# GNN edge stage on one Trainium2 core: gather indices copied mid-pair behind a tile-sum wait, first edge layer for two quads at once

## The chip, the cores and the metric

One core of a Trainium2 chip. The metric is the device time of one launch in microseconds (us), lower is better; it is the median of several runs. One execution was also taken by the hardware profiler. The core's engines run side by side, each with an instruction queue of its own, and meet only at semaphores: TensorE (PE; its weight loads are shown apart as PEld), VectorE (DVE), ScalarE (ACT), GpSimd (POOL) and SyncE (SP, which only issues DMA transfers). "Queue" rows such as ACTq or SPq are DMA issues of that engine.

## The reference

A graph layer over N = 12,500 nodes of 160 features (64 scalars, 32 vectors of 3) and E = 400,000 edges sorted by destination, then a residual and a layer norm. Everything is float32. What costs time are the edges:

```python
h_s, h_v = (node features) @ lin1                       # per node, (12500, 160) in all
w  = silu(edge_scalars @ fc_w1 / 8) @ fc_w2 / 8         # per edge: 64 -> 64 -> 224
es, ev = h_s[edge_src], h_v[edge_src]                   # gather of 160 values per edge
m_s1 = w1 * es * e0                                     # products of w, the gathered row
m_s2 = w4 * einsum('eci,ei->ec', ev, e1) / sqrt(3)      # and the edge's four attributes
m_v1, m_v2, m_v3 = (w2*es) x e1, w3*ev*e0, w5*cross(ev, e1)
agg = segment_sum(messages, edge_dst)                   # per node
out = layernorm(x + gated(lin2(agg) + sc(x)))
```

## The kernel before

The program has three blocks, one after the other. The set-up block computes the table of transformed node rows (`m.h`) in HBM and prepares constants. The edge block goes over all edges and leaves sums per destination window in `m.agg`. The node block turns these into the output. The change touches the edge block alone.

**Tiles, quads, pairs.** Edges are padded to 3128 tiles of 128. Four tiles are a quad (`QT = 4`, 782 quads), two quads a pair (391 pairs), four pairs a round of the ring (`RING = 8` quads of buffers for gathered rows; `ROUNDS = 97` rounds and a rest of six quads). Nothing is scheduled automatically: each engine's queue is the order in which its function below is written, with waits on counting semaphores.

**GpSimd** (`pair`, L543 to L555) works by pairs. It waits until the products of the pair that used these ring slots before are done (`prod_ready`), copies the 8 columns of source indices of the pair into `idx` (L549), waits for that copy's own semaphore `idx_ready`, and issues eight indirect gathers of 128 rows x 160 values (L553), each into one tile's slot of `rows`.

**TensorE** (`turn`, L777 to L784) works by quads q: `hidden(q + 2)` is the first edge layer (L744, 128 x 256: two tiles stand on the upper half of the partitions and two on the lower, with a block-diagonal `fc1`), into its half b of PSUM tile `psx`; `weights(q + 1)` is the second layer (L753, two products of 480 columns) into `psw[b]`; `combine(q - 1)` (L772, L774) adds the tile sums of two quads into one window (`psg`); `sum_tiles(q)` (L762) sums products over the edges of a tile into eight destinations (`pst`). It takes quad q's products and so waits for `prod_ready`, and ends with `tiles_summed`.

**ScalarE** (`turn`, L607 to L613) applies silu to `psx` (L590, `hid`), issues the load of the edge features two quads on into the half of `es` that is free (L584), copies the combined window out of PSUM (L600, `aggsb`) and the tile sums (L605, `tsum`).

**VectorE** (`products`, L660 to L679) waits for the second layer (`w_ready`) and for the quad's four gathers (`rows_loaded`), and multiplies them (L480, L490, L491 into `prod`); it also makes the selection matrices (`sel`, `hot`, `shifts`). **SyncE** stores the windows to HBM.

In the edge block, each fp32 matmul stands as two records in the trace. At the block's beginning ScalarE also issues eight loads of the edge columns `e_cols` (L620), between the first loads of `es` and the ones after it.

Of the kernel before, what the change touches and what calls it, by code (L numbers as in the profile page):

```python
# [398 lines left out]
def edge_block(nc, io, m):  # L399

    with ExitStack() as ctx:
# [6 lines left out]
        es = sb("es", [P, 2, CH])  # L408
        hid = sb("hid", [P, 2, CH])
# [19 lines left out]
        psx = ctx.enter_context(nc.psum_tensor("psx", [P, 2, 256], F32))  # L429
# [4 lines left out]
        es_loaded = [sem(f"es_loaded{b}") for b in range(2)]  # L434
# [4 lines left out]
        prod_seen = sem("prod_seen")  # L439
# [54 lines left out]
        def _(sp):  # L494
# [23 lines left out]
            with sp.Else():  # L518
# [5 lines left out]
                def tile(q, u, first):  # L524
                    if not first:
                        sp.wait_ge(g_added, 16 * (QT * q + u))
                        sp.sem_inc(loads_seen, 1)
                    h = S * (u % 2)
                    sp.dma_start(es[0:S, 0, 0:P], io["esP"][h:h + S, ds(q * CH + P * (u // 2), P)]).then_inc(g_es, 16)
                    sp.dma_start(dstrow[:], io["dst"][ds(QT * q + u, 1), :].to_broadcast([P, P])).then_inc(g_dst, 16)  # L530
# [9 lines left out]
        def _(pool):  # L540
            miss = pool.value_load(m.misses[0:1, 0:1], min_val=0, max_val=CHECKS * P)

            def pair(I, v, free):  # L543

                q = I * RING + 2 * v
                if free:
                    pool.wait_ge(prod_ready, q + 2 - RING)
                    pool.sem_inc(prod_seen, 1)
                nc.gpsimd.tensor_copy(idx[:, 2 * QT * v:2 * QT * v + 2 * QT], m.src[:, ds(q * QT, 2 * QT)]).then_inc(idx_ready, 1)  # L549
                pool.wait_ge(idx_ready, RING // 2 * I + v + 1)  # L550
                pool.sem_inc(prod_seen, 1)
                for j in range(2 * QT * v, 2 * QT * v + 2 * QT):
                    nc.gpsimd.indirect_dma_start(  # L553
                        out=rows[:, j, :], out_offset=None, in_=m.h,
                        in_offset=bass.IndirectOffsetOnAxis(ap=idx[:, j:j + 1], axis=0)).then_inc(rows_loaded[j // QT], 16)  # L555

            with pool.If(miss == 0):
                for v in range(RING // 2):
                    pair(0, v, False)
                with pool.Fori(1, ROUNDS) as I:  # L560
                    for v in range(RING // 2):
                        pair(I, v, True)
                for v in range(REST // 2):
                    pair(ROUNDS, v, True)
# [15 lines left out]
        def _(act):  # L580
            miss = act.value_load(m.misses[0:1, 0:1], min_val=0, max_val=CHECKS * P)
            def load(q, b):

                act.dma_start(es[:, b, :], io["esP"][:, ds(q * CH, CH)]).then_inc(es_loaded[b], 16)  # L584
# [22 lines left out]
            def turn(i, b, last, free, ahead, following):  # L607
                q = 2 * i + b
                if ahead:
                    activate(q + 2, b, True, following)  # L610
                if last:
                    copy_out(q - 1, i - 1 + b, 1 - b, free)
                copy_tiles(q, b)  # L613

            with act.If(miss == 0):
                for b in range(2):
                    load(b, b)
# [3 lines left out]
                for b in range(2):  # L621
                    activate(b, b, False, True)
# [12 lines left out]
            with act.Else():  # L635
# [3 lines left out]
                with act.Fori(0, TILES) as t:  # L639
                    act.wait_ge(g_hid, t + 1)  # L640
                    nc.scalar.activation(hid[0:S, 0, 0:P], psx[0:S, 0, 0:P], ACT.Silu,
# [94 lines left out]
        def _(pe):  # L736
            miss = pe.value_load(m.misses[0:1, 0:1], min_val=0, max_val=CHECKS * P)

            def hidden(q, i, b, free):

                pe.wait_ge(es_loaded[b], 16 * (i + 1))
                if free:
                    pe.wait_ge(hid_ready, q)
                nc.tensor.matmul(psx[:, b, 0:CH], m.fc1[:], es[:, b, :], start=True, stop=True).then_inc(hid_summed, 1)  # L744

            def weights(q, b, free):

                pe.wait_ge(hid_ready, q + 1)
                if free:
                    pe.wait_ge(prod_ready, q - 1)  # L750
# [398 lines left out]
```

## Time and profile before

| | |
|---|---|
| median of 3 runs | 4876.2 us (4875.2 to 4877.35) |
| the profiled execution | 4866.93 us |
| its span in the trace | 4865.1 us |
| edge block, first to last gather | 141.75 to 4409.43 us |
| busy: PE, POOL, DVE, ACT | 4238.8, 3066.4, 2525.6, 1760.2 us |

The page gives per engine the busy time and its share of the span; the waits view gives for each group of instructions how long its engine stood idle before it and what ended that idling ("issue" is time in which it waited for nothing that the profile shows); the timeline gives instructions in order of time, each with its start, its duration and, in brackets, the idle time before it and its releaser. Matmuls are pipelined and their ends are modelled, so TensorE's busy time is not its time at full speed; starts of matmuls can be compared with one another.

### The profile page before, as it was taken

The page shows a single profiled execution, that of the slowest core. Times are in us where ns is not written, and L with a number is a line of the kernel's source. Part 1 is how long each engine was busy: PE and PEld are TensorE (multiplying, and loading weights), DVE is VectorE, ACT ScalarE, POOL GpSimd, SP SyncE. Part 2 cuts the span into 40 slices and gives each one's busy share as a digit, 9 for nine tenths or more (in the row PEclk, how much of TensorE's full clock was granted, in tenths as well). Part 3 has the DMA queues.
Part 4 walks back from the last instruction along what each step waited for, and adds up shares of the span by engine and source line. Part 5 has one row for each costly group of instructions (what it writes and reads, how often), then busy time and mean ns, then how long its engine had stood idle before and what let it go on. Part 6 is the DMA issues. An engine that isn't in the chain of part 4 may idle for free. (4 is left out here: it accounts for less than half of the span.)

```text
span 4865.1 us, 80511 instructions
## 1 busy us (share of the span) xinstructions
PE 4238.8 (87%) x17609; PEld 1960.6 (40%) x17609; DVE 2525.6 (52%) x7615; ACT 1760.2 (36%) x5088; POOL 3066.4 (63%) x3529
## 2 busy tenths in 40 slices
PE   9888888888888888888888888888888888888996
PEld 7433333333333333333333333333333333335775
DVE  3455555555555555555555555555555555554556
ACT  2333333333333333333333333333333333332221
POOL 0677777777777777777777777777777777771000
PEclk9999999999999999999999999999999999999998
DMA  5533333333333333333333333333333333333434
GB/s 149 161 101 99 100 99 99 99 100 99 99 100 99 99 100 99 99 99 100 99 99 100 99 99 99 100 99 99 100 99 99 99 100 99 99 100 105 127 115 137
DMA packets 431352, 506.88 MB, mean 104 GB/s; under 512 B 71411, under 2 KB 359568, under 8 KB 430948
## 3 DMA queue, kind: packets, MB, share of 16 engines
q0 software_dynamic: 150144, 256.45, 20.4%
q1 hardware_dynamic: 152658, 133.76, 9.2%
q10 hardware_dynamic: 128530, 116.45, 7.9%
q8 instruction: 7, 0.11, 0.0%
q14 instruction: 13, 0.11, 0.0%
HBM read 426.32 MB, written 80.06 MB: 104 GB/s over the span
## 5 line engine op out<-in xcount | busy, mean ns | idle before, releaser
L553 POOL DMA_INDIRECT rows<-h_table,idx x3128 | 2987.5, 955 | 1201.2 <-issue 881.0
L480 DVE TENSOR_TENSOR prod<-psw,rows 128x384 f32<-128x384 f32 (+2 forms) x3128 | 1213.4, 450 | 1981.3 <-DMA rows<-h_table,idx 1918.5
L600 ACT ACTIVATE aggsb<-psg 32x160 f32<-32x160 f32 x3128 | 923.4, 295 | 2147.4 <-PE psg L774 2117.9
L753 PE MATMUL psw<-fc,hid 128*128 128x480 f32 x3128 | 1418.2, 577 | 0.0
L762 PE MATMUL pst_e<-prod,sel 128*32 128x448 f32 x6256 | 761.1, 559 | 537.3 <-DVE prod L491 537.1
L753 PEld LDWEIGHTS psw<-fc,hid 128*128 128x128 f32 x3128 | 607.5, 194 | 388.1 <-issue 344.7
L772 PE MATMUL psg<-tsum,shifts 128*128 128x448 f32 x1564 | 717.8, 541 | 1.6 <-ACT tsum L605 1.6
L774 PE MATMUL psg<-tsum,shifts 128*128 128x448 f32 x1562 | 715.3, 540 | 0.0
L744 PE MATMUL psx<-es,fc 128*128 128x256 f32 x1564 | 559.0, 440 | 18.6 <-DMA es<-in_esP 15.0
L762 PEld LDWEIGHTS pst_e<-prod,sel 128*32 128x32 f32 x6256 | 123.5, 108 | 1094.6 <-DVE prod L491 1052.8
L605 ACT ACTIVATE tsum<-pst_e 128x448 f32<-128x448 f32 x782 | 425.5, 544 | 348.6 <-PE pst_e L762 328.0
L744 PEld LDWEIGHTS psx<-es,fc 128*128 128x128 f32 x1564 | 237.0, 191 | 601.7 <-issue 585.1
L772 PEld LDWEIGHTS psg<-tsum,shifts 128*128 128x128 f32 x1564 | 300.1, 192 | 341.0 <-issue 337.8
L774 PEld LDWEIGHTS psg<-tsum,shifts 128*128 128x128 f32 x1562 | 297.1, 190 | 290.9 <-issue 290.9
L590 ACT ACTIVATE hid<-psx 128x256 f32<-128x256 f32 x782 | 299.7, 383 | 140.7 <-PE psx L744 96.9
L679 DVE TENSOR_TENSOR shifts<-shift,tile_offset 128x256 f32<-128x256 f32 x782 | 325.2, 416 | 0.0
L490 DVE TENSOR_TENSOR prod<-psw,rows 128x256 f32<-128x256 f32 x782 | 324.5, 415 | 0.0
L491 DVE TENSOR_TENSOR prod<-psw,rows 128x256 f32<-128x256 f32 x782 | 324.4, 415 | 0.0
L670 DVE TENSOR_TENSOR sel<-hot,e_cols 128x128 f32<-128x128 f32 x782 | 228.8, 293 | 53.0
L912 PE MATMUL pst<-ident,nag 128*32 128x128 f32 (+2 forms) x1764 | 186.7, 286 | 17.8 <-DMA nxv<-in_xT 17.0
L549 POOL COPY idx<-src_cols 128x8 int32 (+1 forms) x391 | 77.8, 199 | 141.2 <-issue 139.8
L912 PEld LDWEIGHTS pst<-ident,nag 128*32 128x32 f32 (+2 forms) x1764 | 120.5, 126 | 70.9 <-issue 23.2
(103 smaller groups left out, 1196.8 us busy)
## 6 DMA issues: line engine op xcount, KB each, us to landing
es<-in_esP ACTq DMA_DIRECT2D x782, 128.0 KB, 2.7
agg_table<-aggsb SPq DMA_DIRECT2D x782, 80.0 KB
rows<-h_table,idx POOLq DMA_INDIRECT x3128
nag<-agg_table SPq DMA_DIRECT2D x24, 1280.0 KB, 6.0
h_table<-hrow ACTq DMA_DIRECT2D x24, 320.0 KB, 3.7
nxr<-in_x SPq DMA_DIRECT2D x24, 320.0 KB, 6.7
out<-y SPq DMA_DIRECT2D x24, 320.0 KB
e_cols<-in_e4T ACTq DMA_DIRECT2D x8, 686.0 KB, 9.8
```

Source lines behind the costliest of these rows:

```text
L480: return nc.vector.tensor_tensor(out, w_part, ev, ALU.mult)
L490: nc.vector.tensor_tensor(w2, w[:, :, 0:S].rearrange(halves, c=V), vec[:, :, 0:S].rearrange(halves, c=V), ALU.mult)
L491: return nc.vector.tensor_tensor(out[:, :, V * B1A:V * B1A + S], w[:, :, S + 3 * V:WN], vec[:, :, 0:S], ALU.mult)
L553: nc.gpsimd.indirect_dma_start(out=rows[:, j, :], out_offset=None, in_=m.h, in_offset=bass.IndirectOffsetOnAxis(ap=idx[:, j:j + 1], axis=0 ...
L600: ins = nc.scalar.activation(aggsb[r, b, :], picked(psg[r, :], k), ACT.Copy)
L605: nc.scalar.activation(tsum[:, b, :], pst[b][:, 0:PW], ACT.Copy).then_inc(tsum_copied, 1)
L679: nc.vector.tensor_tensor(shifts[:, b, :, :, :].rearrange("p h k n -> p h (k n)"), m.shift[:].rearrange("p k n -> p (k n)").unsqueeze(1).t ...
L744: nc.tensor.matmul(psx[:, b, 0:CH], m.fc1[:], es[:, b, :], start=True, stop=True).then_inc(hid_summed, 1)
L753: ins = nc.tensor.matmul(both[:, 0:256 + WN], hid[:, b, P * c:P * c + P], m.fc2[:], start=True, stop=True)
L762: ins = nc.tensor.matmul(pst[b][W * j:W * j + W, 0:PW], sel[:, b, j, :, :], prod[:, b, j, :], start=True, stop=True, tile_position=(0, W * j))
L772: ins = nc.tensor.matmul(psg[:, 0:PW], shifts[:, b, 0, :, :], tsum[:, b, :], start=True, stop=not before)
L774: ins = nc.tensor.matmul(psg[:, 0:PW], shifts[:, b, 1, :, :], tsum[:, 1 - b, :], start=False, stop=True)
```

## The change

Two things change together.

On GpSimd, the index copy becomes a step of its own (`copy_indices`). The first pair's indices are copied before everything; those of each later pair are copied in the middle of the pair before it, after its fourth gather. The wait for products (`prod_ready`, of the quad seven back) is replaced by a wait for tile sums: before pair (q, q + 1), `tiles_summed` must have reached q - 2, that is, quad q - 3 must be summed on TensorE. The first two pairs don't wait for it.

The first edge layer handles two quads at once. `es`, `hid` and `psx` are no longer two halves of 256 columns but one piece of 512, numbered by r = q / 2. TensorE's `hidden(r)` is one product of 512 columns, in turns b = 0 only; ScalarE's `activate(r)` is one silu of 512 columns, likewise, and needs the second layer of quad 2r - 1 done, since `hid` has one buffer; one load brings the features of two quads. The second layer, the sums, the combining and all of VectorE stay by quads.

```diff
-        es = sb("es", [P, 2, CH])
-        hid = sb("hid", [P, 2, CH])
+        es = sb("es", [P, 2 * CH])
+        hid = sb("hid", [P, 2 * CH])
...
-            def pair(I, v, free):
-
-                q = I * RING + 2 * v
-                if free:
-                    pool.wait_ge(prod_ready, q + 2 - RING)
-                    pool.sem_inc(prod_seen, 1)
-                nc.gpsimd.tensor_copy(idx[:, 2 * QT * v:2 * QT * v + 2 * QT], m.src[:, ds(q * QT, 2 * QT)]).then_inc(idx_ready, 1)
+            def copy_indices(I, v):
+
+                slots = slice(2 * QT * v, 2 * QT * v + 2 * QT)
+                nc.gpsimd.tensor_copy(idx[:, slots], m.src[:, ds((I * RING + 2 * v) * QT, 2 * QT)]).then_inc(idx_ready, 1)
+
+            def pair(I, v, following, early):
+
+                if not early:
+                    pool.wait_ge(tiles_summed, I * RING + 2 * v - 2)
                 pool.wait_ge(idx_ready, RING // 2 * I + v + 1)
-                pool.sem_inc(prod_seen, 1)
-                for j in range(2 * QT * v, 2 * QT * v + 2 * QT):
+                pool.sem_inc(order_seen, 1)
+                for j in range(2 * QT):
+                    slot = 2 * QT * v + j
                     nc.gpsimd.indirect_dma_start(
...
+                    if following and j == QT - 1:
+                        last = v == RING // 2 - 1
+                        copy_indices(I + 1 if last else I, 0 if last else v + 1)
...
-            def activate(q, b, free, following):
-                act.wait_ge(hid_summed, q + 1)
+            def activate(r, free, following):
+
+                act.wait_ge(hid_summed, r + 1)
                 if free:
-                    act.wait_ge(w_ready, q - 1)
-                nc.scalar.activation(hid[:, b, :], psx[:, b, 0:CH], ACT.Silu, scale=HID ** -0.5).then_inc(hid_ready, 1)
+                    act.wait_ge(w_ready, 2 * r)
+                nc.scalar.activation(hid[:], psx[:], ACT.Silu, scale=HID ** -0.5).then_inc(hid_ready, 1)
                 if following:
-                    load(q + 2, b)
+                    load(r + 1)
...
-                if ahead:
-                    activate(q + 2, b, True, following)
+
+                if ahead and b == 0:
+                    activate(i + 1, True, following)
...
-            def hidden(q, i, b, free):
-
-                pe.wait_ge(es_loaded[b], 16 * (i + 1))
+            def hidden(r, free):
+
+                pe.wait_ge(es_loaded, 16 * (r + 1))
                 if free:
-                    pe.wait_ge(hid_ready, q)
-                nc.tensor.matmul(psx[:, b, 0:CH], m.fc1[:], es[:, b, :], start=True, stop=True).then_inc(hid_summed, 1)
+                    pe.wait_ge(hid_ready, r)
+                nc.tensor.matmul(psx[:], m.fc1[:], es[:], start=True, stop=True).then_inc(hid_summed, 1)
...
-                if hid_following:
-                    hidden(q + 2, i + 1, b, True)
+                q = 2 * i + b
+                if b == 0 and hid_following:
+                    hidden(i + 1, True)
```

GpSimd's queue within the ring loop, the second pair of a round, before (`idx<-src_cols` is the index copy, `rows<-h_table,idx` a gather, REGISTER_ALU and ISA rows are steps of the sequencer):

```order
L547 REGISTER_ALU
L549 ISA [waits prod_ready]
L549 COPY idx<-src_cols 128x8
L550 REGISTER_ALU
L553 DMA rows<-h_table,idx 128x160 [waits idx_ready]
L553 DMA rows<-h_table,idx 128x160 x7
```

and the same pair now:

```order
L552 REGISTER_ALU [waits tiles_summed]
L556 DMA rows<-h_table,idx 128x160 [waits idx_ready]
L556 DMA rows<-h_table,idx 128x160 x3
L546 ISA
L546 COPY idx<-src_cols 128x8
L556 DMA rows<-h_table,idx 128x160 x4
```

The copy has moved from directly ahead of the gather that waits for it to five places ahead of the next pair's first gather, and both waits now stand together at the beginning of the pair.

TensorE's queue in its loop, the turn b = 0 and the beginning of b = 1, before (`psx` first layer, `psw` second, `psg` combining, `pst_e` tile sums):

```order
L743 ISA [waits es_loaded0]
L744 MATMUL psx<-es,fc 128x256 [waits hid_ready]
L753 MATMUL psw<-fc,hid 128x480 [waits prod_ready,hid_ready]
L753 MATMUL psw<-fc,hid 128x480
L771 REGISTER_ALU [waits shifts_ready,tsum_copied]
L772 MATMUL psg<-tsum,shifts 128x448 [waits agg_copied]
L774 MATMUL psg<-tsum,shifts 128x448
L758 REGISTER_ALU
L762 MATMUL pst_e<-prod,sel 32x448 [waits tsum_copied,prod_ready]
L762 MATMUL pst_e<-prod,sel 32x448 x3
L743 REGISTER_ALU [waits es_loaded1]
L744 MATMUL psx<-es,fc 128x256 [waits hid_ready]
```

and now:

```order
L749 REGISTER_ALU [waits es_loaded]
L750 MATMUL psx<-es,fc 128x512 [waits hid_ready]
L756 REGISTER_ALU [waits hid_ready]
L760 MATMUL psw<-fc,hid 128x480 [waits prod_ready]
L760 MATMUL psw<-fc,hid 128x480
L778 REGISTER_ALU [waits shifts_ready,tsum_copied]
L779 MATMUL psg<-tsum,shifts 128x448 [waits agg_copied]
L781 MATMUL psg<-tsum,shifts 128x448
L765 REGISTER_ALU
L769 MATMUL pst_e<-prod,sel 32x448 [waits tsum_copied,prod_ready]
L769 MATMUL pst_e<-prod,sel 32x448 x3
L756 ISA [waits hid_ready]
```

The turn b = 0 begins with one product of 512 columns, and the turn b = 1 begins with the second layer directly.

## Rows read from the trace of the kernel before

**Rows 1.** The page's busy time, share of the span and instructions of each engine.

```profile
PE 4238.8 (87%) x17609; PEld 1960.6 (40%) x17609; DVE 2525.6 (52%) x7615; ACT 1760.2 (36%) x5088; POOL 3066.4 (63%) x3529
```

**Rows 2.** The page's granted TensorE clock in 40 slices, in tenths of full.

```profile
PEclk9999999999999999999999999999999999999998
```

**Rows 3.** Waits: engine, tile, line, releaser: us in total, times, longest.

```profile
DVE prod L480 <- DMA rows<-h_table,idx: 1918.5, 759, 4.5
POOL rows L553 <- issue: 881.0, 2735, 1.7
POOL rows L553 <- POOL idx L549: 319.7, 391, 1.0
POOL rows L553 <- DVE prod L491: 0.6, 2, 0.3
```

**Rows 4.** GpSimd's timeline at a pair's end: start us, duration us, [idle before].

```profile
2500.46 0.97 POOL L553 DMA_INDIRECT rows<-h_table,idx  x1 [0.82 <-POOL idx L549]
...
2510.18 0.20 POOL L549 COPY idx<-src_cols 128x8 int32 x1
2511.19 0.97 POOL L553 DMA_INDIRECT rows<-h_table,idx  x1 [0.81 <-POOL idx L549]
2512.46 0.95 POOL L553 DMA_INDIRECT rows<-h_table,idx  x1 [0.30 <-issue]
```

**Rows 5.** GpSimd's timeline: first pairs, a rare gap, the last gather.

```profile
141.75 0.19 POOL L549 COPY idx<-src_cols 128x8 int32<-128x8 int32 x1 [139.78 <-issue]
...
151.84 0.94 POOL L553 DMA_INDIRECT rows<-h_table,idx  x1 [0.30 <-issue]
...
163.51 0.20 POOL L549 COPY idx<-src_cols 128x8 int32<-128x8 int32 x1
...
2458.52 0.94 POOL L553 DMA_INDIRECT rows<-h_table,idx  x1 [1.67 <-issue]
...
4408.44 0.99 POOL L553 DMA_INDIRECT rows<-h_table,idx  x1 [0.30 <-issue]
```

**Rows 6.** Timeline of VectorE and TensorE behind the gather that ends at 2510.18.

```profile
2511.88 1.55 DVE L480 TENSOR_TENSOR prod<-psw,rows 128x384 f32<-128x384 f32 x4 [2.33 <-DMA rows<-h_table,idx]
...
2514.15 0.96 PE L762 MATMUL pst_e<-prod,sel 128*32 128x448 f32 x8 [0.42 <-DVE prod L491]
```

**Rows 7.** TensorE's timeline at the start of the edge block.

```profile
161.94 1.22 PE L744 MATMUL psx<-es,fc 128*128 128x256 f32 x2 [8.86 <-DMA es<-in_esP]
...
170.84 0.96 PE L762 MATMUL pst_e<-prod,sel 128*32 128x448 f32 x8
171.72 0.70 PE L744 MATMUL psx<-es,fc 128*128 128x256 f32 x2
172.26 1.77 PE L753 MATMUL psw<-fc,hid 128*128 128x480 f32 x4
173.87 0.92 PE L772 MATMUL psg<-tsum,shifts 128*128 128x448 f32 x2
...
175.47 0.96 PE L762 MATMUL pst_e<-prod,sel 128*32 128x448 f32 x8
```

**Rows 8.** Timeline of GpSimd and TensorE after another rare gap.

```profile
2586.51 0.96 PE L762 MATMUL pst_e<-prod,sel 128*32 128x448 f32 x8 [2.80 <-DVE prod L491]
2587.13 0.20 POOL L549 COPY idx<-src_cols 128x8 int32 x1
2588.13 3.27 PE L753 MATMUL psw<-fc,hid 128*128 128x480 f32 x4
2592.84 0.96 PE L762 MATMUL pst_e<-prod,sel 128*32 128x448 f32 x8
```

**Rows 9.** Window there: us, PE busy (records), granted clock, DMA share, GB/s.

```profile
2585.00:2590.00 5.00, 3.49 (x13) 0.77 0.31 80
```

**Rows 10.** The page's group of silu, and its DMA issue of edge features.

```profile
L590 ACT ACTIVATE hid<-psx 128x256 f32<-128x256 f32 x782 | 299.7, 383 | 140.7 <-PE psx L744 96.9
es<-in_esP ACTq DMA_DIRECT2D x782, 128.0 KB, 2.7
```

More of the change, by code:

```diff
@@ L433, in edge_block @@
         e4_loaded = sem("e4_loaded")
-        es_loaded = [sem(f"es_loaded{b}") for b in range(2)]
+        es_loaded = sem("es_loaded")
         hid_summed = sem("hid_summed")
@@ L607, in turn @@
             def turn(i, b, last, free, ahead, following):
-                q = 2 * i + b
-                if ahead:
-                    activate(q + 2, b, True, following)
+                if ahead and b == 0:
+                    activate(i + 1, True, following)
                 if last:
-                    copy_out(q - 1, i - 1 + b, 1 - b, free)
-                copy_tiles(q, b)
+                    copy_out(2 * i + b - 1, i - 1 + b, 1 - b, free)
+                copy_tiles(2 * i + b, b)
             with act.If(miss == 0):
-                for b in range(2):
-                    load(b, b)
+                load(0)
                 for q in range(E4_PIECES):
@@ L620, in _ @@
                     act.dma_start(m.e4[:, tiles, :], io["e4T"][:, tiles, :]).then_inc(e4_loaded, 16)
-                for b in range(2):
-                    activate(b, b, False, True)
+                activate(0, False, True)
                 for b in range(2):
@@ L640, in _ @@
                     act.wait_ge(g_hid, t + 1)
-                    nc.scalar.activation(hid[0:S, 0, 0:P], psx[0:S, 0, 0:P], ACT.Silu,
+                    nc.scalar.activation(hid[0:S, 0:P], psx[0:S, 0:P], ACT.Silu,
                                          scale=HID ** -0.5).then_inc(g_act, 1)
@@ L775, in combine, with turn @@
                 ins.then_inc(quad_summed, 1)
-            def turn(q, i, b, first, hid_following, w_following):
-                if hid_following:
-                    hidden(q + 2, i + 1, b, True)
+            def turn(i, b, first, hid_following, w_following):
+                q = 2 * i + b
+                if b == 0 and hid_following:
+                    hidden(i + 1, True)
                 if w_following:
-                    weights(q + 1, 1 - b, not (first and b == 0))
+                    weights(i + b, 1 - b, not (first and b == 0))
                 if b or not first:
@@ L803, in _ @@
                         pe.wait_ge(g_es, 16 * (t + 1))
[L804 removed]
+                        nc.tensor.matmul(psx[:, 0:P], m.fc1[0:S, :], es[0:S, 0:P], start=True, stop=True).then_inc(g_hid, 1)
                         pe.wait_ge(g_act, t + 1)
[L806 removed]
+                        nc.tensor.matmul(psw[0][:, 0, 0:WN], hid[0:S, 0:P], m.fc2[0:S, 0:WN], start=True, stop=True).then_inc(g_w, 1)
                         pe.wait_ge(g_prod, t + 1)
```

43 lines of the change are left out of this document (21 added, 22 removed).

## Prediction, written before the changed kernel was run

> **What bounds the kernel now.** I read four views in this order. The busy totals [rows 1] point at TensorE: 87% of the span against 63% for GpSimd. But a matmul's end is modelled, so a busy TensorE may still be waiting, and the waits view settles the matter [rows 3]. VectorE waits 1918.5 us, 759 times, for gathered rows, that is, for nearly every one of the 782 quads. GpSimd, which issues the gathers, waits 0.6 us in all for the products that free its buffers. What it calls idle is only "issue" (881.0 us, 2735 times) and its own index copy (319.7 us, 391 times). So GpSimd never stands still for anybody, and everybody stands still for GpSimd.
>
> The GpSimd timeline gives the beat [rows 4]. A gather takes 0.95 us and the next one starts 0.30 us after it: 1.25 us per gather. At the end of a pair the index copy (0.20 us) starts with no gap at all after the eighth gather, but the first gather of the next pair starts only 0.81 us after the copy ends. From first gather to first gather (2500.46 to 2511.19) a pair takes 10.73 us. The whole stream runs from 141.75 to 4409.43 [rows 5], 4267.7 us for 391 pairs, or 10.91 us each. The difference of 0.18 us has two small parts: one gap of 1.67 instead of 0.30 us on each of 35 occasions, 88 gathers apart (48 us in all, 0.12 per pair; one is in [rows 5]), and an eighth gather that takes some 0.05 us longer (0.99 at 4408.44). The set-up before and the node stage after (from about 4420) are not touched.
>
> **Part 1: the copy moves to the middle of the pair.** Nothing is removed from GpSimd: 3128 gathers and 391 copies remain. What goes is the wait between a copy and the gather behind it. Each gather needs 0.30 us before it starts, even behind another gather; so of the 0.81 us, 0.51 us is the round trip of the copy's own semaphore. With the copy four gathers ahead, that semaphore has been up for about 5 us when it is asked for. The first gather after the wait also takes 0.97 instead of 0.95 us. The new pair: 8 x 1.25 + 0.20 = 10.20 us, plus the 0.05 us of the gather ahead of the copy and 0.12 us for the rare gaps, 10.37 us. Saved per pair: 0.51 + 0.02 = 0.53 us; the first pair keeps its wait, so 390 x 0.53 = 207 us.
>
> Two gaps of the new order are not in the trace: from the copy to the fifth gather (no wait between), and from the eighth gather over two satisfied waits and a register step to the next pair's first. For each, the nearest rows are 0.30 us (gather to gather) and 0.81 us (copy, wait, gather). I take 0.30 for both: the copy itself starts at 0.00 us behind a wait, a semaphore increment and a register step that are already satisfied, so the sequencer works ahead during a gather. If a tenth of a microsecond sticks in one of them, that is 39 us; if 0.51 us does, the gain is gone. Downwards: were the copy to hide wholly in the 0.30 us, another 0.20 x 390 = 78 us would go. The copy's zero gap speaks against it, since the 0.30 us seems to belong to the start of a gather.
>
> Here a rule speaks against the change. Gathers with VectorE idle (151.84 us) and with it busy (2512.46) take the same 0.94 to 0.95 us [rows 4, 5]. The Trainium skill (GPSIMD Engine Reference, Key points) says that GpSimd shares its SBUF interfaces with VectorE and contends with VectorE instructions that have two SBUF inputs; a denser VectorE would then stretch gathers, and if a tenth of the gain were lost by it the time would be 20 us longer. The trace shows such stretching at most in the 0.05 us of each eighth gather, and I give it nothing.
>
> **Part 2: the new wait.** Before each pair, GpSimd now waits for the tile sums of the second quad of the pair two back. Behind it in GpSimd's queue are all gathers, so a late sum stops the bounding engine. In steady state it has room: the last gather of a pair ends at 2510.18, VectorE takes up its rows at 2511.88, the sums run from 2514.15 to 2515.11 [rows 4, 6], 4.93 us after the gather. The pair that asks starts a whole pair plus 0.30 us after that gather, so the room is 10.25 + 0.30 - 4.93 = 5.6 us. Around a rare gap the sums come later: gathers done at 2587.13, sums at 2593.80 [rows 8], 6.7 us, which leaves 3.9 us. Cost: nothing, while TensorE keeps up.
>
> At the start it does not. The second edge-feature load queues behind the eight loads of edge columns, TensorE waits 8.86 us and starts the next first-layer product at 161.94 only; the sums of quad 1 end at 171.80 (170.84 + 0.96) [rows 7]. Today GpSimd issues its third pair at 163.51 + 0.20 + 0.81 = 164.5 regardless [rows 5]. In the new kernel that pair needs this sum. Its natural start is about 163.5; the sum comes a little later than 171.8, since the product there took 1.22 us at the low clock and is now twice as wide: up to 173.0. I put the wait's end in the middle, at 172.4: it costs 9 us (bounds 7 and 12). It is paid once, since TensorE then does two quads in 9.1 us against GpSimd's 10.2.
>
> **Part 3: two quads at once.** TensorE in a catch-up stretch, when its rows are there, shows its own pace [rows 7]: sums at 170.84 and again at 175.47, 4.63 us per quad, of which 0.54 us is the first-layer product (171.72 to 172.26). A record of 480 columns takes 0.40 us ((173.87 - 172.26) / 4), so two records of 512 columns take 0.86 us, at most twice 0.54. TensorE's pair is then 2 x 4.63 - 2 x 0.54 + 0.86 = 9.04 us (up to 9.26), in turns of 4.95 and 4.09 us where the gathers bring quads every 5.0 and 5.2. The long turn just fits; if it runs 0.1 late the short one makes it good. Silu takes 0.383 us for 256 columns [rows 10], so at most 0.77 for 512. It can start once the weights of the second quad are done, while TensorE goes on with the 1.60 us of combining (173.87 to 175.47) and the next sums, so it is not waited for. There is one buffer now for the features instead of two: the load is issued with the silu, some 7 us before its use, and landed in 2.7 us at 128 KB [rows 10]; even doubled it is in time. All of this lies beside the gathers, so it gains and costs nothing: ACT issues 391 loads fewer, TensorE 391 products fewer, none on the path.
>
> **The sum.** 4876.2 - 207 + 9 = 4678 us. The profiled execution took 4866.93 us (span 4865.1), 9 us below the median; its own sum is 4669. Scaling would not change the difference, so I set the forecast against the median: 4678 us, 4.1% faster.
>
> **The rivals.**
> - *The wait only changes its place.* The 0.51 us stays at the pair's boundary or behind the copy. For it: two waits and a register step now stand directly ahead of a gather, which no row of before shows. Against: the copy's zero gap. Saved 0.02 x 390 = 8, paid 9: 4877 us, no change. Chance 0.06.
> - *TensorE becomes the bound.* Its turns at full clock need 9.04 to 9.26 us of 10.2; it would take a stall of over 1 us per pair, for example by silu waiting for the weights while TensorE waits for silu. At 10.6 us per pair: 4678 + 391 x 0.25, some 4780 us. Chance 0.05. For it: only 0.1 us of room in the long turn, and one hidden buffer instead of two.
> - *The new wait binds, and the kernel is slower.* The mechanism: TensorE's granted clock falls to its lower level, sums come late, GpSimd stops, rows come late, TensorE idles again. The trace has falls: after 2.80 us of idling the window from 2585 shows a clock of 0.77 [rows 8, 9], and the second-layer products take 3.27 us instead of 1.77 [rows 7, 8]. At the low level I take 18 us per pair (1.85 times the products' time, and a little for idling). If a share s of time is spent there, a pair takes 9.15 + 8.85 s, over GpSimd's 10.2 from s = 0.12 and over today's 10.91 from s = 0.20, a mean clock of 0.90. At s = 0.25: 11.4 us per pair, about 5050 us. Against: today's falls follow idling, the slices of the edge stage all show 9 tenths or more [rows 2], and a faster GpSimd leaves TensorE less idle. The Trainium skill (TensorE: Matmul & The Clock Gate, What's actually happening) says the same way that throttled is the default and activity releases it; by it the clock would rise rather than fall. Chance 0.06.
> - *The copy hides.* 4678 - 78 = 4600 us. Chance 0.03.
>
> **How the numbers follow.** The forecast has 0.80, with its own range of 4655 (a tenth of a microsecond better per pair, or a cheaper start) to 4725 (a tenth lost at one of the two gaps and 10 us more at the start). What misses the range beside it is 0.20, from the rivals. The range of 4650 to 4735 holds the forecast's case whole and some of the cases between it and TensorE's. A measurement tells about 0.2%, 10 us. Faster: 0.80 + 0.05 + 0.03 = 0.88; within 0.2%: 0.06; slower: 0.06.
>
> **What would show it.** In the profile of the changed kernel: the GpSimd timeline with 10.2 us per ordinary pair, 0.30 us behind the copy and at the pair's boundary (step 1); GpSimd's waits with one wait of about 9 us for tile sums near 163 us and none of note later (step 2); a first-layer product and a silu every other quad, near 0.9 us and below 0.8, and VectorE still waiting for rows in nearly every quad (step 3); the node stage starting about 198 us earlier. The prediction is wrong if the boundary gap is nearer 0.8 than 0.3, if GpSimd shows repeated waits for sums, or if VectorE's waits name the second-layer product instead of the rows.

## The result: 4602 us, 5.6% faster, below the range that was forecast

| | before | after |
|---|---|---|
| median | 4876.8 us (4875.2 to 4877.8, 4 runs) | 4602.0 us (4601.6 to 4605.0, 4 runs) |
| profiled execution, span | 4866.9, 4865.1 us | 4601.6, 4599.8 us |
| ratio | | 0.9439, 95% interval 0.9428 to 0.9450 |

Forecast were 4678 us and a range of 4650 to 4735. The direction was right; the gain is 275 us instead of 198. The place is right too: the stream of gathers takes 4001.6 us (142.61 to 4144.17) instead of 4267.7, 266 us less, and the node stage behind it is as long as it was.

In two of the sets of runs below every kernel was slower, the kernel before too (6319 and 6454 us, with waits whose releaser the traces call "remote"), and three kernels (medians 4849.6, 4578.3 and 4606.1 us) had one run of four that took 0.7 to 1.1 ms longer; no cause is read from such times.

The page's busy time of the changed kernel, and then its waits (engine, tile, line, releaser: us in total, times, longest), against [rows 1, 3]:

```profile
PE 4176.6 (91%) x16827; PEld 1792.1 (39%) x16827; DVE 2529.0 (55%) x7615; ACT 1706.0 (37%) x4697; POOL 3093.8 (67%) x3529
```

```profile
DVE prod L480 <- DMA rows<-h_table,idx: 1082.9, 516, 9.7
POOL rows L556 <- issue: 834.4, 2743, 0.3
...
DVE prod L480 <- PE psw L760: 628.5, 265, 12.3
...
POOL rows L556 <- POOL idx L546: 63.1, 382, 1.0
```

GpSimd's idling behind its own copy has fallen from 319.7 to 63.1 us. Its "issue" idling has lost its longest case: 0.3 us instead of 1.7. VectorE waits for rows in 516 quads and for TensorE's second layer in 265, where it was rows nearly always.

GpSimd's timeline from a pair's fourth gather to the copy in the next pair (the boundary lies between the gathers at 2489.72 and 2490.97), against [rows 4]:

```profile
2484.60 0.98 POOL L556 DMA_INDIRECT rows<-h_table,idx  x1 [0.30 <-issue]
2485.58 0.20 POOL L546 COPY idx<-src_cols 128x8 int32 x1
2485.94 0.97 POOL L556 DMA_INDIRECT rows<-h_table,idx  x1 [0.16 <-POOL idx L546]
2487.22 0.95 POOL L556 DMA_INDIRECT rows<-h_table,idx  x1 [0.30 <-issue]
2488.47 0.94 POOL L556 DMA_INDIRECT rows<-h_table,idx  x1 [0.30 <-issue]
2489.72 0.95 POOL L556 DMA_INDIRECT rows<-h_table,idx  x1 [0.30 <-issue]
2490.97 0.95 POOL L556 DMA_INDIRECT rows<-h_table,idx  x1 [0.30 <-issue]
...
2495.71 0.20 POOL L546 COPY idx<-src_cols 128x8 int32 x1
```

From copy to copy 10.13 us instead of 10.73. The boundary costs 0.30 us like any gap between gathers, as assumed. Behind the copy stand 0.16 us, where 0.30 was assumed. And the eighth gather of before, which averaged 1.00 us and took up to 1.18, has company now: the fourth, behind which the copy stands, takes 0.98 here and 0.99 and 1.15 in the next two pairs.

The start, against [rows 5, 7]:

```profile
162.88 0.95 POOL L556 DMA_INDIRECT rows<-h_table,idx  x1 [0.30 <-issue]
173.71 0.94 POOL L556 DMA_INDIRECT rows<-h_table,idx  x1 [9.89 <-PE pst_e L769]
```

The new wait costs 9.6 us there (9.89 less the usual 0.30), and nothing later: GpSimd's waits name tile sums three times, 10.4 us in all.

The two timelines, taken together over all pairs from the seventh on (mean us per pair), say where the rest of the gain is:

| part of a pair | before | after | difference |
|---|---|---|---|
| end of the eighth gather to the next first | 1.019 (with copy) | 0.305 | |
| end of the fourth gather to the fifth | 0.305 | 0.365 (with copy) | together -0.65 |
| end of the first gather to the second | 0.429 (35 times 1.67) | 0.305 | -0.12 |
| the eight gathers themselves | 7.64 | 7.71 | +0.07 |
| the whole pair | 10.916 | 10.208 | -0.71 |

390 x 0.71 - 9.6 = 267 us, and 266 are measured. The medians differ by some 9 us more than the streams: the profiled execution of before lay 10 us below the median of before, and that of after did not. No trace shows what those 10 us are.

### The profile page after: what moved, and what is told of

It reads as the page before. It is cut to its first block and busy times, and to the rows that moved or that the text cites. A ratio compares the mean times of both kernels' runs of the same rounds, so it can differ in the third digit from the quotient of the medians.

```text
span 4599.8 us, 77581 instructions
## 1 busy us (share of the span) xinstructions
PE 4176.6 (91%) x16827; PEld 1792.1 (39%) x16827; DVE 2529.0 (55%) x7615; ACT 1706.0 (37%) x4697; POOL 3093.8 (67%) x3529
## 5 line engine op out<-in xcount | busy, mean ns | idle before, releaser
L769 PE MATMUL pst_e<-prod,sel 128*32 128x448 f32 x6256 | 750.9, 552 | 333.5 <-DVE prod L491 331.8
L760 PEld LDWEIGHTS psw<-fc,hid 128*128 128x128 f32 x3128 | 563.0, 190 | 810.2 <-issue 805.0
L598 ACT ACTIVATE hid<-psx 128x512 f32<-128x512 f32 x391 | 233.5, 597 | 831.4 <-PE psw L760 831.4
L750 PE MATMUL psx<-es,fc 128*128 128x512 f32 x782 | 441.9, 647 | 17.1 <-DMA es<-in_esP 17.1
L750 PEld LDWEIGHTS psx<-es,fc 128*128 128x128 f32 x782 | 116.7, 188 | 303.4 <-issue 284.7
```

The lines of the kernel that those rows point to most:

```text
L750: nc.tensor.matmul(psx[:], m.fc1[:], es[:], start=True, stop=True).then_inc(hid_summed, 1)
L760: ins = nc.tensor.matmul(both[:, 0:256 + WN], hid[:, at:at + P], m.fc2[:], start=True, stop=True)
L769: ins = nc.tensor.matmul(pst[b][W * j:W * j + W, 0:PW], sel[:, b, j, :, :], prod[:, b, j, :], start=True, stop=True, tile_position=(0, W * j))
```

## The experiments

The theories: **A**, the gain is GpSimd's alone, and its size is that of the round trip of the copy's semaphore plus the rare gaps; **B**, the two-quad layer has a part in it (half the loads, a lighter TensorE). Two questions remained beside them: why are the 35 rare gaps gone, and why do gathers take longer?

**GpSimd's part alone**, on the kernel before:

```diff
-                    pool.wait_ge(prod_ready, q + 2 - RING)
...
+                    pool.wait_ge(tiles_summed, I * RING + 2 * v - 2)
...
+                    if following and j == QT - 1:
+                        copy_indices(...)        # first layer, es, hid, psx: unchanged
```

> Only GpSimd's part of the change: copy in the middle of the pair, wait for tile sums; the first layer stays quad by quad with two buffers. Theory A (the gain is GpSimd's alone): a pair takes 10.2 us as in the changed kernel, the 35 rare gaps of 1.37 us stay away, the start costs some 9 to 10 us; 4602 us, within 8. Rival B (the rare gaps went because half the edge-feature loads are gone, and TensorE at 9.3 us per pair is helped by the double width): the rare gaps come back, 48 us, and GpSimd is stopped now and then; 4650 us or more.

Measured: 4605.8 us, ratio 0.9443 (0.9427 to 0.9459). The gain is here, to within the interval of the changed kernel's own ratio (0.9428 to 0.9450); the pair takes 10.22 us and past the start no gap between gathers exceeds 0.31 us away from the copy. B falls as the source of the gain.

**The two-quad layer alone**, GpSimd as before:

> Only the two-quad first layer; GpSimd as before (copy at the pair's start, wait for products). Theory A: the GpSimd stream is as before, 10.91 us per pair with 35 gaps of 1.67 us; 4876 us, within 5. Rival B: the rare gaps are gone with half the feature loads, 4828 us.

Measured: 4866.5 us, ratio 0.9976 (0.9967 to 0.9986). Its gather stream is that of before to 0.2 us (4267.9 us, 35 gaps of 1.67), and its profiled execution took 4869.1 us, 2 us more than that of before. So the traces show no gain. The medians do show one, of 12 us (0.24%) and clear of the noise. It is about as large as the unexplained 10 us between profile and median of before, but no run tells whether the two are the same; beside GpSimd's part the two-quad layer brings 4 us, within the noise. That much stays open for B.

**The wait one pair looser:**

```diff
-                    pool.wait_ge(tiles_summed, I * RING + 2 * v - 2)
+                    pool.wait_ge(tiles_summed, I * RING + 2 * v - 4)
...
-                    pair(0, v, True, v < 2)
+                    pair(0, v, True, v < 3)
```

> The changed kernel with the wait for tile sums one pair looser (the pair three back instead of two back). Theory A: the wait costs only the 9.6 us at the start; with it gone the pairs are the same 10.2 us, 4592 us. Rival C (holding GpSimd close to TensorE keeps the later stages smooth, or took the rare gaps away): the steady pair gets longer or the gaps return, 4602 us or more (4650 with the gaps).

Measured: 4592.8 us, ratio 0.9414 (0.9398 to 0.9430), 9.3 us below the changed kernel. The stream of gathers is 6.9 us shorter (3994.7 us): the 9.6 us of the start are back, and the gathers are 0.007 us per pair longer. The new wait's price is its start; no gap shows anything that it buys.

**The round trip put back**, in the middle of the pair:

```diff
                         copy_indices(I + 1 if last else I, 0 if last else v + 1)
+                        pool.wait_ge(idx_ready, RING // 2 * I + v + 2)
+                        pool.sem_inc(order_seen, 1)
```

> The changed kernel, with GpSimd waiting for its own copy right behind it, before the fifth gather. It brings the round trip back and nothing else. Theory A1 (round trip 0.65 us per pair, and the rare gap is the sequencer's, hidden when it works ahead and shown when a wait for the own copy holds it): 4602 + 391 x 0.65 = 4856 us plus 48 for the rare gaps, 4904 us, gaps of 1.67 us behind a gather every 88. Theory A2 (the rare gap has to do with where the pair begins, not with the wait): 4856 us, no rare gaps.

Measured: 4849.6 us, ratio 0.9941 (0.9921 to 0.9961). GpSimd's timeline:

```profile
2509.80 0.20 POOL L546 COPY idx<-src_cols 128x8 int32 x1
2510.82 0.97 POOL L556 DMA_INDIRECT rows<-h_table,idx  x1 [0.81 <-POOL idx L546]
```

0.81 us instead of 0.16, on 390 pairs: 0.65 x 390 = 254 us, and 248 are measured. That is the gain's main term, produced by one wait. No rare gap came, so a wait for the own copy is not enough for it.

**Where the copy stands.** Copies on VectorE, behind the eighth, behind the seventh gather, and the other wait in the kernel before; all four fell into the first of the two sets in which the kernel before was slower too:

> The changed kernel with the index copies on VectorE, two pairs ahead (at the beginning of each even quad's products); GpSimd issues gathers only, and waits for the products of seven quads back and for the indices, both long there. If the copy's price on GpSimd is what the trace shows (0.20 copy, 0.16 gap instead of 0.30, a fourth gather 0.09 longer and a fifth 0.02: 0.17 us per pair) and TensorE follows (9.4 us of 10.0 per pair), a pair takes 10.03 us: 4602 - 390 x 0.17 - 9.6 at the start = 4526 us. Rival: TensorE or VectorE becomes the bound, since VectorE already waits for the second layer in 265 quads; a pair stays near 10.2 us, 4590 us.

> The changed kernel with the copy behind the eighth gather instead of the fourth, so directly ahead of the wait of the next pair. Theory A (what counts is one gather or more between copy and wait): the whole round trip comes back, 4850 us, as with the wait in the middle of the pair. On the rare gaps: if they go with a copy directly ahead of a pair's first gather, they come back, gathers 88 apart, and it is 4898 us; if they go with the wait for products, which the changed kernel has no more, they stay away, 4850 us.

> The changed kernel with the copy behind the seventh gather: one gather (1.25 us) lies between the copy and its wait. Theory A: the round trip of some 0.65 us is shorter than that gather, so it is hidden as well as from the middle, 4602 us within 4. Rival: the wait is only free when the sequencer can pass it well ahead, and part of the 0.65 us shows, 4650 to 4750 us.

> The kernel before with one wait exchanged: GpSimd waits for the tile sums of the pair three back instead of the products of seven quads back; the copy stays at the pair's start. If the rare gaps go with the copy's place, nothing changes, 4877 us with 35 gaps. If they go with the wait for products, 4829 us without gaps.

Their times were 5816, 5621, 5601 and 5696 us beside 6319. All four traces have the 35 rare gaps, each after the same gathers (the 113th and every 88th after it), even where GpSimd copies nothing. In this set GpSimd was held at the beginning of many pairs (2.9 to 3.4 us on average from the eighth gather to the next first), which turned out to matter (below), so the fourth kernel's question, whether the kind of wait decides, is not answered by it. Two were repeated and one was added in a set at the usual pace:

```diff
-                    if following and j == QT - 1:
+                    if following and j == 2 * QT - 1:    # and 2 * QT - 2, and 1
```

> The copy behind the eighth gather, once more for the same reason. The round trip is back (0.65 us per pair) and the rare gaps too, as the trace showed: 4602 + 254 + 48 = 4904 us; without the gaps 4856.

> The copy behind the seventh gather, once more. Theory A: a gather of 1.25 us covers the round trip of 0.65 us, so only the rare gaps, which the trace showed, are added: 4602 + 48 = 4650 us. Rival: part of the round trip shows at the pair's boundary, up to 4850 us.

> The changed kernel with the copy behind the second gather instead of the fourth. The wait is covered by six gathers. So far the rare gaps are absent in all kernels that copy behind the fourth gather and present in all others (copy at the pair's start, behind the seventh or the eighth, or on VectorE). Theory D1 (any copy within the pair, away from its ends, takes the event in): no gaps, 4602 us. Theory D2 (only the place behind the fourth does, four gathers from the gap's place): 35 gaps, 4650 us.

| copy behind | time | ratio | rare gap (35 times) |
|---|---|---|---|
| eighth gather | 4882.3 us | 1.0016 (1.0006 to 1.0025) | 1.67 us |
| seventh | 4634.4 us | 0.9507 (0.9492 to 0.9523) | 1.05 us (0.94 to 1.17) |
| fourth (the change) | 4602.0 us | 0.9439 (0.9428 to 0.9450) | none |
| second | 4592.2 us | 0.9421 (0.9405 to 0.9437) | none |

One gather between the copy and its wait hides the round trip whole: the boundary gap is 0.305 us with the copy behind the seventh. The rare gap shrinks with the distance. The first row also answers the question left open above: that kernel waits for tile sums, not for products, and has the rare gaps all the same, so the kind of wait is not what removed them. GpSimd's timeline at one of them, copy behind the eighth and then behind the seventh gather:

```profile
3194.38 0.20 POOL L546 COPY idx<-src_cols 128x8 int32 x1
3195.39 0.97 POOL L556 DMA_INDIRECT rows<-h_table,idx  x1 [0.81 <-POOL idx L546]
3198.03 0.95 POOL L556 DMA_INDIRECT rows<-h_table,idx  x1 [1.67 <-issue]
```

```profile
3012.07 1.02 POOL L556 DMA_INDIRECT rows<-h_table,idx  x1 [0.16 <-POOL idx L546]
3013.40 0.95 POOL L556 DMA_INDIRECT rows<-h_table,idx  x1 [0.30 <-issue]
3015.36 0.94 POOL L556 DMA_INDIRECT rows<-h_table,idx  x1 [1.02 <-issue]
```

With the copy behind the seventh, its semaphore comes up about 0.5 us after the copy's end (0.81 - 0.30), that is some 0.67 us before the eighth gather ends; and the rare gap here is 0.65 us shorter. My reading is that the gap is what is left of a pause after GpSimd's queue has used up its lead over the gathers; it is tested below. (The copy behind the second gather gains 10 us more, and all of it is in the gathers' own lengths: 10.18 us per pair.)

**The copies on VectorE**, two pairs ahead, at the usual pace. This kernel also waits for the products of seven quads back instead of the tile sums, and so has no wait of 9.6 us at the start:

```diff
-                    pool.wait_ge(tiles_summed, I * RING + 2 * v - 2)
+                    pool.wait_ge(prod_ready, I * RING + 2 * v + 2 - RING)
...
+            def copy_indices(I, v):
+
+                nc.vector.tensor_copy(idx[:, 2 * QT * v:2 * QT * v + 2 * QT],
+                                      m.src[:, ds((I * RING + 2 * v) * QT, 2 * QT)]).then_inc(idx_ready, 1)
...
+                if b == 0 and copied:
+                    copy_indices(I + (u + 4) // RING, (u + 4) % RING // 2)
```

> The kernel with the index copies on VectorE once more, for a comparison at the pace of the first profiles: in the four runs before, all four queues stopped together for some us at a time and the kernel before took 6319 us, so their times say nothing about a copy. Their traces did show the 35 rare gaps, also here, where GpSimd copies nothing. So: pair of 10.03 us plus 0.12 for the gaps; 4602 + 48 - 66 - 10 = 4574 us. Rival: TensorE becomes the bound, 4600 us or more.

Measured: 4578.3 us, ratio 0.9386 (0.9367 to 0.9405), the fastest kernel here that computes the whole result. But the parts were not the expected ones: no rare gaps, and a pair of 10.17 us instead of 10.03, since the fourth and eighth gathers take 1.03 and 1.01 us although no copy stands beside them. So the copy does not lengthen them, as I had put it. Of the 24 us by which it beats the changed kernel some 10 are the start's and 15 the pair's. TensorE keeps up.

**The pause.** A wait for the copy placed at a set distance ahead of the rare gap's place:

```diff
-                    if following and j == QT - 1:
+                    if following and j == 2 * QT - 2:    # the other kernel: j == 0
                         copy_indices(...)
+                        pool.wait_ge(idx_ready, RING // 2 * I + v + 2)
+                        pool.sem_inc(order_seen, 1)
```

> The changed kernel with the copy behind the seventh gather and GpSimd's wait for it right behind, ahead of the eighth. Theory S (the rare event is a pause of GpSimd's sequencer between the first and second gather of a pair, hidden as far as the sequencer is ahead of the gathers; a wait for the own copy takes its lead away, and each gather since gives back 1.25 us): two gathers lie between wait and event instead of one, so 1.37 - 1.25 = 0.12 us shows and the gap is 0.42 us instead of 1.67; 4850 + 4 us. Rival A2 (it goes with the copy's or the wait's place at the pair's beginning alone): no gap beyond 0.31.

> The changed kernel with the copy behind the first gather and GpSimd's wait for it right behind, ahead of the second. By theory S the event lies just where the sequencer has no lead: the gap from copy to second gather is 0.81 us as always and longer 35 times, by 1.37 to 2.62 us (nothing, if the pause lies ahead of the wait and is served while the first gather runs); 4850 + 48 to 92 us. Rival A2: no rare gap, 4850 us.

Measured: 4881.8 us (1.0006, 0.9997 to 1.0016) and 4900.0 us (1.0047, 1.0030 to 1.0064). GpSimd's timeline at a rare gap, the wait behind the seventh gather and then behind the first:

```profile
3188.29 1.02 POOL L556 DMA_INDIRECT rows<-h_table,idx  x1 [0.81 <-POOL idx L546]
3189.62 0.95 POOL L556 DMA_INDIRECT rows<-h_table,idx  x1 [0.30 <-issue]
3191.53 0.94 POOL L556 DMA_INDIRECT rows<-h_table,idx  x1 [0.96 <-issue]
```

```profile
3201.87 0.21 POOL L546 COPY idx<-src_cols 128x8 int32 x1
3205.05 0.97 POOL L556 DMA_INDIRECT rows<-h_table,idx  x1 [2.97 <-issue]
```

What stands out over the usual gap is 2.16 us with no gather between wait and pause (2.97 - 0.81), 1.37 us with one (as before), 0.78 us on average with two (0.66 here), and nothing with five or more. Each gather gives back 0.6 to 0.8 us, not the 1.25 that I expected. The theory holds in kind and not in size. (That the lead grows by what a gather takes longer to run than to hand out would explain it, but no row shows the handing out.) That the rare gap goes with the pair's beginning alone is out.

**Longer gathers.** In the traces of both kernels every gather over 1.00 us past the first pair runs beside VectorE's `sel`. Without `hot` and `sel`, so with the selections of the first two quads throughout:

```diff
+                if select:                    # the first two quads alone
                     nc.vector.tensor_tensor(sel[...], hot[...], m.e4[...], ALU.mult)
```

> The changed kernel without VectorE's making of hot and sel after the first two quads (its output is wrong for that: the selection matrices stay those of quads 0 and 1); all else is unchanged. In the traces so far every gather over 1.00 us runs beside sel. Theory F (VectorE operations with two inputs in SBUF stretch a gather that they fall into): the fourth and eighth gather go back to 0.95 us, a pair takes 10.21 - 0.12 = 10.09 us, 4602 - 46 = 4556 us. Rival G (the stretching comes from the semaphores of the quad or the loads and stores that start then): the long gathers stay, 4602 us within 5.

Measured: 4606.1 us, ratio 0.9443 (0.9424 to 0.9462). My expectation was wrong: nothing was gained. But each of the long gathers (350 over 1.00 us past the first pair) now stood beside `shifts`, which also reads two tensors in SBUF. VectorE's and GpSimd's timeline in this kernel:

```profile
2504.00 0.42 DVE L686 TENSOR_TENSOR shifts<-shift,tile_offset 128x256 f32<-128x256 f32 x1
2504.11 1.12 POOL L556 DMA_INDIRECT rows<-h_table,idx  x1 [0.30 <-issue]
```

So `shifts` went too (a memset of one element in its place), and in another kernel alone:

> The changed kernel without VectorE's making of hot, sel and shifts after the first two quads (a memset of one element stands in place of shifts; the output is that of stale selections). Without hot and sel alone the long gathers stayed, all of them now beside shifts. Theory F (any VectorE operation with two inputs in SBUF stretches a gather): with the last of them gone all gathers take 0.95 to 0.97 us, 4602 - 40 = 4562 us. Rival G (something else of that moment does it, such as the semaphores or the start of the tile sums' reads): the fourth gather stays at 1.04 us or more, 4602 us.

> The changed kernel without shifts alone (the same memset in its place); hot and sel are made as ever. Theory F: hot and sel move some 0.3 us earlier and still fall into or between gathers, so part of the stretching stays, beside sel alone: between 4562 and 4602 us. Rival G: 4602 us, and long gathers with no overlap with sel.

> The kernel without hot, sel and shifts once more (stale selections, so its output is wrong). In the run before, the queues stopped together and the kernel before took 6454 us, so gathers and VectorE did not keep their usual places; it had 1 gather over 1.00 us in 3128. With them at their usual places: theory F, 0.95 to 0.97 us for every gather, a pair of 10.09 us and 4562 us; rival G, 1.04 us for the fourth gather and 4602 us.

The first two fell into the second of the two sets in which the kernel before was slower too (5688 and 5603 us beside 6454), where gathers and VectorE don't keep their places; they had 1 and 18 gathers over 1.00 us. The third decides: 4550.9 us, ratio 0.9330 (0.9314 to 0.9345). The page's group of gathers, in the changed kernel and without the three operations (x count | busy us, mean ns | idle us before, releasers):

```profile
L556 POOL DMA_INDIRECT rows<-h_table,idx x3128 | 3014.4, 964 | 907.8 <-issue 834.4 <-POOL idx L546 63.1 <-PE pst_e L769 10.4
```

```profile
L556 POOL DMA_INDIRECT rows<-h_table,idx x3128 | 2966.8, 948 | 907.2 <-issue 835.0 <-POOL idx L546 63.0 <-PE pst_e L773 9.2
```

47.6 us of GpSimd's busy time gone, the idle time before gathers the same to 1 us, 51 us of the kernel's time gone; 10.085 us per pair. One gather over 1.00 us is left, the first of all. A long case in the changed kernel:

```profile
2504.77 0.41 DVE L685 TENSOR_TENSOR shifts<-shift,tile_offset 128x256 f32<-128x256 f32 x1
2504.86 1.15 POOL L556 DMA_INDIRECT rows<-h_table,idx  x1 [0.30 <-issue]
...
2505.10 0.22 DVE L662 TENSOR_TENSOR hot<-win,dst_in_window 128x64 f32<-128x64 f32 x1
2505.46 0.29 DVE L676 TENSOR_TENSOR sel<-hot,e_cols 128x128 f32<-128x128 f32 x1
```

The products, which read PSUM and SBUF and take far more of VectorE's time, lengthen nothing: 1355 gathers of the changed kernel stand beside products alone, with a mean of 0.945 us and 0.957 at most.

To stand beside is not enough, though. VectorE's and GpSimd's timeline in the kernel before:

```profile
2502.98 0.94 POOL L553 DMA_INDIRECT rows<-h_table,idx  x1 [0.30 <-issue]
2503.00 0.41 DVE L491 TENSOR_TENSOR prod<-psw,rows 128x256 f32<-128x256 f32 x1
2503.33 0.42 DVE L679 TENSOR_TENSOR shifts<-shift,tile_offset 128x256 f32<-128x256 f32 x1
2503.66 0.22 DVE L656 TENSOR_TENSOR hot<-win,dst_in_window 128x64 f32<-128x64 f32 x1
2504.01 0.29 DVE L670 TENSOR_TENSOR sel<-hot,e_cols 128x128 f32<-128x128 f32 x1
2504.23 0.95 POOL L553 DMA_INDIRECT rows<-h_table,idx  x1 [0.30 <-issue]
```

`shifts` and `hot` begin inside the first gather, and it takes the usual time; `sel` runs on only 0.07 us into the second. Counted over whole traces past the first pair: all 373 gathers over 1.00 us of the changed kernel, and all 168 of the kernel before, began while one of the three operations was running. Where one only began during a gather (207 and 477 gathers), none took over 0.97 us. In the kernel with `shifts` alone of the three, a `shifts` that ends some 0.21 us into a gather goes with 1.03 us, and one that ends 0.31 us into it with 1.13 us: what it lasts beyond the gather's first 0.13 us is added whole.

## Why the prediction was right, and where it was wrong

**The bound** was read rightly. GpSimd's stream set the time before, and what was taken out of it came out of the kernel (266 us of the stream, and 265 of the span of the profiled executions). The kernel without the two-quad layer has the same gain, to 4 us.

**Part 1, the round trip.** The mechanism was right, and this is where the forecast failed: three terms of its sum were mis-sized. (a) The gap behind the copy: 0.30 us was taken from gather to gather, 0.16 is measured. This is 0.14 x 390 = 55 us more. My reason, that the whole 0.30 us belongs to the start of a gather, fails for 0.14 of it. Whether these pass beside the copy or belong to the gather that has just ended, no run tells. The rival "the copy hides" had the right sign with a bound of 0.20, and I had given it a chance of 0.03 and left it outside my range. That its 4600 us is nearly the measured time is luck: 55 of its 78 us came, and the rest is made up by the two terms below. (b) The rare gaps were carried over as 0.12 us per pair without a reason. They went with the wait ahead of them: 35 x 1.37 = 48 us. The row was at hand: 1.67 us always behind the first gather after a wait, where the queue has no lead. (c) Gathers beside VectorE: I gave this nothing and even booked 0.02 us of gain; measured are 0.07 us per pair the other way, 0.09 x 390 = 35 us against. Here the Trainium skill (GPSIMD Engine Reference, Key points) was the better guide: by its rule VectorE operations with two SBUF inputs contend with GpSimd. The traces agree, in the long gathers and in the run without these operations (48 us), with the limit that such an operation counts only where a gather begins during it. No run has a VectorE operation with one SBUF input of such a length, so that it takes two of them is not shown apart from there being no PSUM. I had compared gathers beside the products, which read one input from PSUM, and so looked at the wrong operation. The sum: 55 + 48 - 35 = 68 us, by which the stream gained more than forecast (266 us instead of 198). The time missed by 76; the other 8 are the open difference between profile and median of before.

**Part 2, the new wait** was right to a microsecond: 9.6 us paid once (9 said), waits for tile sums of no note later, and 9.3 us back with the wait one pair looser. Two small errors met in it: the wait ended at 173.71 instead of 172.4, and the third pair would have begun at 164.1 instead of 163.5. That the first product there ran at the lower clock, as I had written, is not recorded in the trace of before; in the trace of GpSimd's part alone the granted clock is 0.50 from 157 to 166 us, the lower level.

**Part 3, two quads at once** was right for the streams: no gain, no loss. TensorE's and ScalarE's timeline of one pair, against [rows 7]:

```profile
2474.33 0.96 PE L769 MATMUL pst_e<-prod,sel 128*32 128x448 f32 x8 [0.88 <-DVE prod L491]
...
2475.22 1.12 PE L750 MATMUL psx<-es,fc 128*128 128x512 f32 x2
...
2476.18 1.77 PE L760 MATMUL psw<-fc,hid 128*128 128x480 f32 x4
...
2477.99 0.60 ACT L598 ACTIVATE hid<-psx 128x512 f32<-128x512 f32 x1 [2.09 <-PE psw L760]
...
2479.44 0.96 PE L769 MATMUL pst_e<-prod,sel 128*32 128x448 f32 x8
...
2484.48 0.96 PE L769 MATMUL pst_e<-prod,sel 128*32 128x448 f32 x8 [0.77 <-DVE prod L491]
```

The first layer takes 0.96 us (0.86 said, 1.08 as the bound), so the long turn is 5.11 us, just what the gathers leave it, and the short one idles 0.77 us. Silu starts once the weights are through, and TensorE waits for it for 1.7 us in all. What I had not seen is that VectorE would now wait for the second layer in a third of the quads. "VectorE still waiting for rows in nearly every quad" did not come true, and waits naming the second layer were among my signs of being wrong. The sign was ill chosen: with the first layer quad by quad VectorE waits for rows 774 times again, and that kernel is no faster (4605.8 us), so these waits cost nothing; but they show how close TensorE has come.

**The rivals.** The wait did not move to the boundary. TensorE did not become the bound. The clock did not fall: its mean rose from 0.983 to 0.994. The rule of the clock gate that I had cited from the Trainium skill (TensorE: Matmul & The Clock Gate, What's actually happening) points the same way. What moved it was the rare gaps: in the edge block before, the granted clock fell to its lower level (1.2 GHz) 25 times, each time 7 to 9 us after the gather behind a rare gap began, beside a TensorE idle time of 2.75 to 2.93 us. With the wait behind the first gather, where the rare gaps are longest, it fell 28 times; in the changed kernel it did not fall there past the start, and neither did it with the wait put back in the middle of the pair, which has the slow pair but no rare gap. **The range** was the second fault: it was built around small terms carried over unchanged, and the two largest that moved moved the same way.

## What to carry to other kernels

On the engine that bounds, put an instruction whose result the same queue waits for at least one of its neighbours ahead: here 1.25 us of distance hid a round trip of 0.65 us, 254 us in all. (Three gathers more of distance brought another 32 us, most of it from the rare gaps.) A queue that waits on itself also loses its lead, and shows pauses that it would otherwise hide, so small regular gaps behind such a wait should be counted as part of its price. And look at what the other engines are doing as the bounding engine's slightly longer instructions begin, before giving them no weight.

## What the runs showed of the hardware

- An index copy on GpSimd in front of a gather that doesn't wait for it costs 0.20 + 0.16 - 0.30 = 0.06 us; with a wait for it 0.71 us.
- GpSimd's stream of indirect gathers has a pause after its 113th gather and every 88th after that, the same in all kernels that show it. It is over 2 us long (2.16 seen where the queue has just waited) and cannot be seen where the queue has been free for five gathers. What it is stays open.
- Behind such a pause TensorE's clock can fall: 25 falls to the lower level behind 35 rare gaps in the kernel before, and none past the start in the kernels without such gaps.
- A VectorE operation with two SBUF inputs that is running when a gather of 0.95 us begins lengthens it, up to 1.20 us; removing these operations saved 48 us of 3014 us of gathers. One that begins during a gather did not (477 gathers before, 0.97 us at most), nor did products with one input in PSUM.
